# A graph attention kernel in which VectorE makes half of the scatters' one-hot matrices itself

## The reference, cut to what matters

```python
q = qkv[:, 0] * SCALE
k = qkv[:, 1]
v = qkv[:, 2]
scores = jnp.einsum('ehd,ehd->eh', q[src], k[dst])
m = jax.ops.segment_max(scores, dst, num_segments=n)
e = jnp.exp(scores - m[dst])
s = jax.ops.segment_sum(e, dst, num_segments=n)
sa = e / s[dst]
he = (v[src] * sa[:, :, None]).reshape(-1, D)
agg = jax.ops.segment_sum(he, dst, num_segments=n)
```

## Time and profile before

| | us |
|---|---|
| median of 3 runs | 3458.22 |
| lowest and highest | 3452.4, 3460.26 |
| the profiled execution | 3463.14 |
| its span in the trace | 3461.3 |

### The profile page before, as it was taken

The page is one execution under the profiler, slowest core; times in us unless marked ns, Lnnn a source line. Parts: engine busy times, 40 slices in busy tenths (PEclk is TensorE's granted clock), DMA queues, the critical chain, the costliest instruction groups (busy, mean ns, idle before and its releaser), DMA issues. The chain is left out here.

```text
span 3461.3 us, 52327 instructions
## 1 busy us (share of the span) xinstructions
PE 2908.6 (84%) x13207; PEld 1895.7 (55%) x13207; DVE 2195.4 (63%) x4818; ACT 968.3 (28%) x2518; POOL 1591.7 (46%) x1665
## 2 busy tenths in 40 slices
PE   3676899999999999949997999999677788777775
PEld 2343555555555555539995888888333333333332
DVE  5675788888888888768863222222555555555555
ACT  0442344444444444446662333333000000000000
POOL 0113767777777777300000000000577777777774
PEclk7787999999999999869998999999877766777676
DMA  1434877777777777433314444444633333333334
GB/s 51 137 126 156 240 227 231 232 229 231 232 231 228 232 226 232 119 124 106 109 44 165 193 190 184 193 187 177 211 105 105 105 105 105 105 105 105 105 105 144
DMA packets 233805, 557.05 MB, mean 161 GB/s; under 512 B 48397, under 2 KB 128353, under 8 KB 220994
## 3 DMA queue, kind: packets, MB, share of 16 engines
q0 software_dynamic: 104144, 324.24, 32.6%
q1 hardware_dynamic: 111706, 197.31, 15.7%
q10 hardware_dynamic: 17688, 32.15, 2.6%
HBM read 402.88 MB, written 150.70 MB: 160 GB/s over the span
## 5 line engine op out<-in xcount | busy, mean ns | idle before, releaser
L1196 POOL DMA_INDIRECT rel_rows<-msg_d,msg_i_again x783 | 743.6, 950 | 851.9 <-DMA msg_i_again<-msg_i_d 613.7
L773 POOL DMA_INDIRECT qv_rows<-qv_d,src_i x832 | 798.5, 960 | 351.0 <-issue 166.1
L1216 PE MATMUL rel_ps<-rel_rows,rel_hot 128*128 x1664 | 759.6, 572 | 235.6 <-SPq L1184 176.6
L1216 PEld LDWEIGHTS rel_ps<-rel_rows,rel_hot 128*128 128x128 f32 x1664 | 355.2, 257 | 639.7 <-issue 630.5
L1052 PE MATMUL out_ps<-qv_rows,hot 128*128 128x264 f32 x1664 | 591.2, 438 | 31.5 <-DVE qv_rows L851 17.1
L1241 DVE TENSOR_TENSOR sums_all<-sums_all,rel_ps 128x256 f32 x832 | 350.4, 421 | 400.8 <-PE rel_ps L1216 346.5
L1737 PE MATMUL ms_mm<-wrel,ms_hTs 128*128 128x512 f32 x2352 | 560.7, 397 | 2.8 <-DVE wrel L1684 2.7
L1737 PEld LDWEIGHTS ms_mm<-wrel,ms_hTs 128*128 128x128 f32 x2352 | 440.7, 189 | 103.0 <-issue 3.3
L933 ACT COPY at_acc<-out_ps 128x264 f32 x832 | 315.5, 379 | 609.6 <-PE out_ps L1052 597.3
L1007 PE MATMUL kx<-k,hot_t 128*128 x2496 | 357.2, 279 | 35.8 <-DVE qv_rows L797 27.3
L1696 DVE TENSOR_TENSOR msg<-ms_mm,ms_gate 128x512 f32<-128x512 f32 x196 | 135.5, 692 | 317.5 <-PE ms_mm L1737 317.5
(11 more groups left out here) (198 smaller groups left out, 2635.4 us busy)
## 6 DMA issues: line engine op xcount, KB each, us to landing
msg_d<-msg SPq DMA_DIRECT2D x98, 1024.0 KB, 3.9
dl_b<-dlt_d ACTq DMA_DIRECT2D x50, 512.0 KB
qv_rows<-qv_d,src_i POOLq DMA_INDIRECT x832, 3.9
qv_d<-qv SPq DMA_DIRECT2D x7, 1820.0 KB, 6.3
rel_rows<-msg_d,msg_i_again POOLq DMA_INDIRECT x783, 2.8
agg_d<-at_acc SPq DMA_DIRECT2D x49, 132.0 KB
up_agg<-agg_d SPq DMA_DIRECT2D x7, 924.0 KB, 4.9
xg<-in_x_dram SPq DMA_DIRECT2D x7, 896.0 KB, 9.3
```

The source lines that it names most:

```text
L773: nc.gpsimd.indirect_dma_start(rows[:, n % SLOTS, :], None, qv_d, bass.IndirectOffsetOnAxis(ap=src_i[:, n:n + 1], axis=0)).then_inc(got[n ...
L1196: nc.gpsimd.indirect_dma_start(rows[:, at:at + FEAT], None, table, bass.IndirectOffsetOnAxis(ap=msg_i[:, e:e + 1], axis=0)).then_inc(got[e ...
L1216: nc.tensor.matmul(sum_ps[n % BANKS][:], hot[:, n % HOTS, :], rows[:, bass.ds(at, FEAT)], start=True, stop=True).then_inc(summed, 1)
```

## The change

Of the four groups of `hot` in a chunk only the first two (`TURNED`) are still transposed by TensorE and copied by ScalarE. The third and the fourth are made by VectorE: `scatter_places` compares `iota_n` (0 to 127 along the columns, the same for each of four steps) with `dloc` (one number for each partition and step) for equality and writes 128x512 floats of `hot`. It waits until the scatters of the chunk before have used that group, and TensorE's scatters 8 and 12 of each chunk wait for it through a semaphore of its own, `hotv_ok`. On VectorE the third group's comparison stands between the values and the places, the fourth's between the third and the fourth head sums. `dloc` is kept through the attention stage, and the ring of `hot_t` is cut from three chunks to two.

```diff
-HOT_RING = 3
+HOT_RING = 2
+TURNED = 2
...
+            dloc = sb(att, "dloc", [P, STEPS])
             with ExitStack() as prep:
-                dloc = sb(prep, "dloc", [P, STEPS])
...
                     if k >= HOT_RING:
-                        dve.wait_ge(turned, QUADS * (k - HOT_RING + 1))
+                        dve.wait_ge(turned, TURNED * (k - HOT_RING + 1))
...
+                def scatter_places(k, quad):
+                    s0 = quad * QUAD
+                    if k >= 1:
+                        dve.wait_ge(summed, UNROLL * (k - 1) + s0 + QUAD)
+                    nodes = iota_n[:].rearrange("p (s n) -> p s n", s=1).to_broadcast([P, QUAD, P])
+                    own_nodes = dloc[:, UNROLL * k + s0:UNROLL * k + s0 + QUAD].rearrange("p (s n) -> p s n", n=1).to_broadcast([P, QUAD, P])
+                    nc.vector.tensor_tensor(hot[:, s0:s0 + QUAD, :], nodes, own_nodes, ALU.is_equal).then_inc(hotv_ok, 1)
...
                         for quad in range(1, QUADS):
                             values(k - 1, quad)
+                        scatter_places(k - 1, 2)
                     if k + 1 < ROUNDS:
                         places(k + 1)
                     if now:
                         product(k, 6)
                         product(k, 7)
                         head_sums(k, 2)
+                    if before:
+                        scatter_places(k - 1, 3)
+                    if now:
                         head_sums(k, 3)
...
-                        turned_back(k - 1, 2)
                         evacuate(k - 1, banks, 4)
                         evacuate(k - 1, banks, 5)
-                        turned_back(k - 1, 3)
...
-                        pe.wait_ge(hotf_ok, QUADS * k + s // QUAD + 1)
+                        if s // QUAD < TURNED:
+                            pe.wait_ge(hotf_ok, TURNED * k + s // QUAD + 1)
+                        else:
+                            pe.wait_ge(hotv_ok, (QUADS - TURNED) * k + s // QUAD - TURNED + 1)
...
-                    if before:
-                        turn_hot(k - 1, 2)
                     if now:
                         expand(k, tiles, 5)
...
                         clear(early(4))
-                        step = early(5)
-                        turn_hot(k - 1, 3)
-                        clear(step)
+                        clear(early(5))
```

More of the change, by code:

```diff
@@ L137, in gnn_program @@
                             (dloc, norm_s, msg_i), late_d, msg_i_d, late_st)
-            attention(nc, sb, ps, sem, qv_d, agg_d, dlt_d, brk_d, fl_d, hb_d, k3, ident, ident_b, ones, part,
+            attention(nc, sb, ps, sem, qv_d, agg_d, dlt_d, brk_d, fl_d, hb_d, k3, ident, ident_b, iota_n, dloc, ones, part,
                       src_i, end_i, tab, got)
@@ L679, in _, with attention @@
                         last.then_inc(ends_tr, 1)
-def attention(nc, sb, ps, sem, qv_d, agg_d, dlt_d, brk_d, fl_d, hb_d, k3, ident, ident_b, ones, part,
+def attention(nc, sb, ps, sem, qv_d, agg_d, dlt_d, brk_d, fl_d, hb_d, k3, ident, ident_b, iota_n, dloc, ones, part,
               src_i, end_i, tab, got):
@@ L695, in attention @@
     shift_ok, exp_ok, p_ok, resc_ok, val_ok = (sem(f"at_{n}") for n in ("shift", "exp", "p", "resc", "val"))
-    turned, hotf_ok, summed, cleared, init_ok, own = (sem(f"at_{n}") for n in ("turned", "hotf", "sum", "clear", "init", "own"))
+    turned, hotf_ok, hotv_ok, summed, cleared, init_ok, own = (sem(f"at_{n}") for n in ("turned", "hotf", "hotv", "sum", "clear", "init", "own"))
     acc_ok, acc_st, stored, turn = (sem(f"at_{n}") for n in ("acc", "accs", "stored", "turn"))
@@ L897, in turned_back @@
                 def turned_back(k, i):
-                    act.wait_ge(turned, QUADS * k + i + 1)
+                    act.wait_ge(turned, TURNED * k + i + 1)
                     if k >= 1:
@@ L1018, in turn_hot @@
                 def turn_hot(k, i):
-                    if QUADS * k + i >= 1:
-                        pe.wait_ge(hotf_ok, QUADS * k + i)
+                    if TURNED * k + i >= 1:
+                        pe.wait_ge(hotf_ok, TURNED * k + i)
                     for q in range(QUAD):
```

## The result

The changed kernel takes 3466.4 us (median of 22 runs, 3460.0 to 3471.8), the kernel before, run beside it, 3458.5 us (22 runs, 3449.8 to 3469.4). The ratio is 1.0021, 95% interval 1.0014 to 1.0028: some 7 us slower. The profiled execution took 3471.17 us, with a span of 3469.3.

The account below looks back on a forecast made before the run. The prediction took a chain alternating between VectorE, TensorE and ScalarE, with the dl_b load's wait, to bound each attention chunk. Its terms 4.2 + 0.6 − 1.0 − 0.4 gave +3.4, rounded to +3: 3461 us, range 3449 to 3484.

Parts of the forecast that it names:

- The class with the largest chance: Whole kernel: same time as before, within about 0.2% (6.9 us); chance 0.58, against slower 0.29 and faster 0.13.
- The price of a comparison: VectorE, attention stage: each 128x512 comparison adds 0.61 us, bounds 0.58 and 0.98.
- The first comparison hides behind the load of dl_b: VectorE, between values and places: covered by the wait for dl_b except in one instance, 0.6 us for the kernel.
- the cover's loss: VectorE ahead of the places: with the dl_b load's cover gone, the first comparison would cost 32 us.
- The second costs what exceeds the wait ahead of the scan: VectorE, between third and fourth head sums: only the excess over the wait ahead of L811 counts, 4.2 us.
- TensorE's relief: Eight transposes and two copies fewer per chunk: gains only 1.0 us at late chunks and 0.4 in the last.
- Rival 2: TensorE's relief reaches VectorE through the wait ahead of the rescaling in half the chunks: 10 us less, 3451; chance 0.15.
- Rival 1: VectorE beside GpSimd's gathers: each comparison costs 0.95 to 0.98 us, +25 us, 3483; chance 0.18, whole or part.
- The page's rule: Trainium skill, SBUF: a two-SBUF-input VectorE instruction contends with a GpSimd instruction reading SBUF, loser blocks fully; sum would be +25.
- the +25: Attention stage: total change in us if gathers disturb the comparisons, second costing 21.4 and first 4.7, with the gains; 3483.
- Rival 3: TensorE idles 0.8 us more a chunk, so the clock falls in a twentieth of the stage: about +25, 3483; chance 0.05.
- The new waits: Comparisons waiting for the previous chunk's scatters, scatters 8 and 12 waiting for comparisons: all over when reached, zero cost.

Follow-up runs that it names:

- e1: Changed kernel with only the third group compared by VectorE, the fourth transposed and copied as before: 3459.6 us, ratio 0.9995.
- e6: Changed kernel with ScalarE's load of dl_b issued earlier, ahead of the load of the breaks: 3436.1 us, ratio 0.9929.
- e7: Kernel before with ScalarE's load of dl_b issued earlier, ahead of the load of the breaks: 3430.9 us, ratio 0.9915.
- e2: Changed kernel with only the fourth group compared, between the head sums, the third transposed and copied as before: 3467.7 us, ratio 1.0024.
- e3: Changed kernel without the comparisons, that half of hot filled once with zeros: 3453.5 us, ratio 0.9977.
- e4: Kernel before with all transposes and copies kept, both comparisons added into a buffer nobody reads: 3464.8 us, ratio 1.0014.
- e9: Kernel before with the earlier dl_b load and only the fourth group's comparison, between the head sums; third group transposed: 3432.0 us, ratio 0.9909.
- e10: Kernel before with the earlier dl_b load, fourth group's comparison between the head sums, third group's ahead of maxima: 3430.7 us, ratio 0.9909.
- e12: Changed kernel with only the third group's comparison, moved ahead of maxima, the fourth transposed and copied as before: 3467.4 us, ratio 1.0019.

## Why the prediction was right or wrong

The forecast was +3 us (3461), range 3449 to 3484; measured were 3466.4 us and about +7 by the ratio. The range held. The sum was 4 us short, and more than half of the measured cost lies where the sum had nothing, so the nearness of the number is in part luck. The class with the largest chance, within 0.2%, was missed by a hair: the ratio is 1.0021, and its interval lies on both sides of 1.002. Step by step:

- **The price of a comparison**, 0.61 us: 0.60 in the timeline. Interpolating between rows of the same kind worked to 2%.
- **The first comparison hides behind the load of dl_b**, 0.6 us in all: right. e1 is at 0.9995. That the load closes the chunk: right, shown by e6 and e7, with TensorE half a us behind it. What the prediction put on the cover's loss, 32 us, was wrong, since it took the gap to be gone with the load. It moves to the scan and pays there: e6 lies 5 us above e7, and the table has that in the part from the scan to the rescaling.
- **The second costs what exceeds the wait ahead of the scan**, 4.2 us: the mechanism is right, the wait went as forecast. In its own part of the chunk it cost 0.05 us, 2.5 us for the stage, with TensorE's relief included. In e2 the same comparison alone is +8 us: the rest is knock-on in the other two parts.
- **What failed** is the assumption, nowhere written in the sum, that the other parts of the chunk only shift. They grew by 0.08 us each. For the one it is the stretch of the two small instructions beside the gathers, shown above, 0.08 × 52 = 4 us. For the other, the places come 5.11 us after the load's issue on average, 5.04 before, a difference within the scatter of the chunks; whether it is real, and from what, is open.
- **TensorE's relief**, −1.4 us: alone it is worth 6 to 8 us (e3), in company with the comparisons nothing measurable (e4). The prediction costed it as an item of a sum, and it isn't one: relief and comparison meet at one wait, of which only the later party counts. Rival 2 (3451) was, without comparisons, close to what e3 shows, but its full form is out: in e9 the four transposes taken from TensorE's stretch without a pause save nothing.
- **Rival 1, the gathers disturb the comparisons**: no, at 674 to 685 ns. The page's rule, which I named beside the +25, has an exception that I left out: a GpSimd instruction that only writes, to which the page counts the making of descriptors by inference. But something of the kind is real and hit other instructions, and the prediction had a sign of it in its rows: the places with 752 to 997 ns. I read them as a reason for or against the comparison's own price and did not ask which other short instructions would be moved against the gathers.
- **Rival 3, the clock**: no; the granted clock from 500 to 1200 us is 1.00 as before.
- **The new waits**: none is seen, as argued: no wait in the trace is ended by a comparison.

Of the versions tried, e7, the kernel before with an earlier load, is the simplest of the fastest: 3430.9 us, 0.85% faster than the kernel before.

## What to carry to other kernels

Give each piece of work that you add the wait that it fills, by name and length, and then look for work that fills the same wait from the other side: the two don't add. Where a DMA closes a loop, ask first whether it can simply be issued earlier; that was worth four times what this change moved, and the change's own cover was only the symptom of a late issue. Before you read a difference of hundredths of a us per round in one profile, see where that execution lies among its kernel's. When the sum of an edit comes near the noise, expect tenths of a microsecond per round from instructions that merely fall elsewhere against a periodic neighbour.

## What the runs showed of the hardware

- Short VectorE copies and tensor_scalar instructions (eight numbers) last 152 to 161 ns, and up to 431 when they begin 0.51 to 0.76 us after the start of an indirect gather that GpSimd issues; scans and comparisons with two inputs in SBUF beside the same gathers don't change (483 to 486 and 674 to 685 ns).
- TensorE's busy time did not tell what its work was worth: at 95% busy (665.4 of 700 us in e7), four small transposes less in a chunk (e9) changed neither the chunk (21.10 and 21.07 us) nor the busy time (667.5 of 700 us), and eight less (e10, 21.09 us) did not change the chunk either. What sets the pace there is open.
- A 512 KB load issued by ScalarE beside the gathers released the places 4.6 to 6.5 us after its issue, 5.04 on average (the kernel before). The 5.18 us of e12 do not stand clear of that scatter.
